# Exact 12-bit halves of the source tiles, one single-pass product for each, in the graph convolutions of a four-layer GNN + expert-FFN kernel; the gated pass's first loads issued one stage earlier

## The reference, cut to what matters

```
def _gcn_conv(h, row, col, norm, W, b, n_nodes):
    h = h @ W.T
    msg = h[row] * norm[:, None]               # norm = dinv[row] * dinv[col]
    out = jax.ops.segment_sum(msg, col, num_segments=n_nodes)
    return out + b
h = relu(_gcn_conv(x, row, col, norm, W1, b1, n_nodes))
h = relu(_gcn_conv(h, row, col, norm, W2, b2, n_nodes))
out = _gcn_conv(h, row, col, norm, W3, b3, n_nodes)
```

```
ei   = concatenate([x[src], edge_attr], axis=-1)        # 256 + 64 wide
core = maximum(ei @ W1 + b1, 0) @ W2 + b2
gate = sigmoid(ei @ Wg + bg)
agg  = segment_sum(gate * core, dst)
```

## Time and profile before

| | |
|---|---|
| median of three runs | 4353.53 us |
| the profiled execution | 4353.69 us, of which 4351.9 us span |
| busy: PE, PEld | 3722.1 us (86%), 2780.0 us (64%) |
| busy: DVE, ACT, POOL | 2239.8 us (51%), 1240.2 us (28%), 1958.0 us (45%) |
| granted TensorE clock, mean | 0.874 |
| convolutions, first product to last weigh | 1931.53 to 2824.52 us |
| gated pass, start of its block | 3094.8 us |

### The profile page before, as it was taken

One profiled execution on the slowest core, in us unless ns is written; L12 is line 12 of the kernel. 1 busy time (PEld: TensorE's weight loads), 2 busy tenths in 40 slices (PEclk: granted clock), 3 DMA queues, 4 the chain that ended last, 5 costly groups with the idle time before them and its releaser, 6 DMA issues. The chain is left out here.

```text
span 4351.9 us, 63004 instructions
## 1 busy us (share of the span) xinstructions
PE 3722.1 (86%) x19067; PEld 2780.0 (64%) x19067; DVE 2239.8 (51%) x6358; ACT 1240.2 (28%) x3588; POOL 1958.0 (45%) x2029
## 2 busy tenths in 40 slices
PE   3999992964887877849999999978899999998796
PEld 2666661543666666836566566554588888887696
DVE  6887787136555543242012122153577777778423
ACT  3777762210000012210000000021455555555331
POOL 2777766777777766740000000024354544442153
PEclk8999995985557577979999999987999999998698
DMA  7887850002333325745545554355455554442466
GB/s 231 240 227 213 229 142 14 9 3 86 106 106 106 105 61 160 233 148 150 152 136 153 149 146 138 110 144 140 146 146 143 143 143 144 144 143 87 150 211 206
DMA packets 424224, 613.68 MB, mean 141 GB/s; under 512 B 149417, under 2 KB 287794, under 8 KB 423634
## 3 DMA queue, kind: packets, MB, share of 16 engines
q1 hardware_dynamic: 310722, 327.46, 26.3%
q0 software_dynamic: 104112, 273.76, 21.7%
q10 hardware_dynamic: 9056, 8.43, 0.6%
HBM read 517.83 MB, written 91.59 MB: 140 GB/s over the span
## 5 line engine op out<-in xcount | busy, mean ns | idle before, releaser
L873 POOL DMA_INDIRECT eg_rows<-t_edge,src_i x416 | 394.1, 947 | 488.4 <-DVE eg_pre L1711 357.5
L1395 PE MATMUL ps<-cv_cells,xn 128*128 128x384 f32 (+2 forms) x1600 | 535.5, 493 | 60.0 <-DMA cv_cells<-t_cells 60.0
L1116 PE MATMUL ps<-sum_hot,sum_rows 128*128 128x128 f32 x1664 | 439.6, 421 | 170.2 <-DVE sum_hot L1095 92.5
L1116 PEld LDWEIGHTS ps<-sum_hot,sum_rows 128*128 128x128 f32 x1664 | 345.1, 294 | 264.8 <-DMA sum_rows<-t_row,src_i 171.3
L279 POOL DMA_INDIRECT t_cells<-times_seen,cell x416 | 414.4, 996 | 170.4 <-issue 126.2
L1395 PEld LDWEIGHTS ps<-cv_cells,xn 128*128 128x128 f32 x1600 | 304.5, 191 | 272.8 <-issue 61.0
L873 POOL DMA_INDIRECT ag_rows<-t_att,src_i x416 | 403.7, 970 | 138.1 <-issue 118.0
L873 POOL DMA_INDIRECT sum_rows<-t_row,src_i x416 | 393.9, 947 | 129.5 <-issue 120.0
L1663 PE MATMUL ps<-eg_w,eg_rT 128*128 128x256 f32 x1664 | 438.7, 386 | 1.9 <-ACT eg_rT L1681 1.9
L1711 DVE TENSOR_TENSOR eg_pre<-ps,eg_rows 128x512 f32<-128x512 f32 x416 | 283.4, 682 | 141.9 <-PE ps L1650 140.8
L1663 PEld LDWEIGHTS ps<-eg_w,eg_rT 128*128 128x128 f32 x1664 | 283.7, 190 | 57.9 <-issue 34.1
(11 more groups left out here) (412 smaller groups left out, 6409.7 us busy)
## 6 DMA issues: line engine op xcount, KB each, us to landing
cv_cells<-t_cells SPq DMA_DIRECT2D x225, 384.0 KB, 3.2
cv_cells<-t_cells SPq DMA_DIRECT2D x75, 448.0 KB, 3.3
xn<-in_L_ffn_W SPq DMA_DIRECT2D x57, 512.0 KB
t_cells<-zeros SPq DMA_DIRECT2D x17, 1664.0 KB
xn<-in_L_ffn_expert_w SPq DMA_DIRECT2D x110, 256.0 KB, 3.7
ag_trow<-t_dst SPq DMA_DIRECT2D x104, 256.0 KB
t_cells<-zeros POOLq DMA_DIRECT2D x8, 1664.0 KB, 23.3
eg_eaT<-in_edge_attr SPq DMA_DIRECT2D x208, 64.0 KB, 3.3
```

The costliest lines, as they stand in the source:

```text
L873: nc.gpsimd.indirect_dma_start(out=rows[:, j, :], out_offset=None, in_=table, in_offset=bass.IndirectOffsetOnAxis(ap=src_i[:, n:n + 1], ax ...
L1116: mm = nc.tensor.matmul(ps[:, j % BANKS, k * EC:(k + 1) * EC], lhs, hot[:, j, :], start=True, stop=True)
L1395: mm = nc.tensor.matmul(ps[:, bank(q, k, half), 0:at.stop - at.start], source(l)[:, s, k * 128:(k + 1) * 128], cells[:, n % CR, at], start ...
```

## The change

In the convolutions:

- ACT copies each source tile into a tile of type float32r (`high`, ring of four), which keeps the upper 12 bits of the mantissa. POOL subtracts that copy from the source tile and writes the rest, also as float32r (`low`). The two parts add up exactly to the value.
- PE multiplies `high` and `low` in turn with the counts, read as float32r; each source tile and quarter has eight products of the program where it had four.
- ACT now does this copy 300 times and its three copies of `cv_shared` between them. The waits for the source tile (`chain`) and for the copy of the shared part move: from PE to ACT, and to the start of quarter 1.
- POOL clears `featT` for layers 1 and 2 in eight pieces, between the subtractions of source tiles 17 to 24.
- `begin` of quarter 1 is 16 and was 14. The halves of the last quarter are 412 and 410 columns wide.

In the gated pass: the six loads of weights and biases and the first four of attributes are issued by SP in `collect_and_project`, behind the sixth store of `t_edge`; the tiles for them are kept through the stage before. The other attribute loads stand written out, where they were a loop.

```
+            high = sb("cv_high", [P, HR, D], F32R, c)      # HR = 4
+            low = sb("cv_low", [P, HR, D], F32R, c)
...
                 def _(pool):
-                    for l in range(LAYERS):
-                        if l > 0:
-                            pool.wait_ge(g.y_ready.sem, g.y_ready.at(NT * l))
-                        nc.gpsimd.memset(featT[:, :, 0:N], 0.0).then_inc(g.table_clear.sem, 1)
+                    nc.gpsimd.memset(featT[:, :, 0:N], 0.0).then_inc(g.table_clear.sem, CLEARS)
+                    for l, q, s, n in all_halves():
+                        pool.wait_ge(g.high_kept.sem, g.high_kept.at(n + 1))
+                        nc.gpsimd.tensor_tensor(low[:, n % HR, :], source(l)[:, s, :], high[:, n % HR, :].bitcast(F32), ALU.subtract).then_inc(g.low_kept.sem, 1)
+                        if l > 0 and q == 0 and CLEAR_AT <= s < CLEAR_AT + CLEARS:
+                            if s == CLEAR_AT:
+                                pool.wait_ge(g.y_ready.sem, g.y_ready.at(NT * l))
+                            c0 = (s - CLEAR_AT) * (N // CLEARS)
+                            nc.gpsimd.memset(featT[:, :, c0:c0 + N // CLEARS], 0.0).then_inc(g.table_clear.sem, 1)
...
                         for k in range(KD):
-                            for half in range(2):
-                                at = part(q, half)
-                                mm = nc.tensor.matmul(ps[:, bank(q, k, half), 0:at.stop - at.start], source(l)[:, s, k * 128:(k + 1) * 128],
-                                                      cells[:, n % CR, at], start=(s == 0), stop=(s == NT - 1))
+                            for which, split in enumerate((high, low)):
+                                if k == 0 and which == 0:
+                                    pe.wait_ge(g.high_kept.sem, g.high_kept.at(v + 1))
+                                elif k == 0:
+                                    pe.wait_ge(g.low_kept.sem, g.low_kept.at(v + 1))
+                                for half in range(2):
+                                    at = part(q, half)
+                                    mm = nc.tensor.matmul(ps[:, bank(q, k, half), 0:at.stop - at.start], split[:, v % HR, k * 128:(k + 1) * 128],
+                                                          cells[:, n % CR, at].bitcast(F32R), start=(s == 0 and which == 0), stop=(s == NT - 1 and which == 1))
...
-                            begin = 14 if q == 1 else 8
+                            begin = 16 if q == 1 else 8
...
                 def _(act):
+                    for l, q, s, n in all_halves():
+                        if n >= HR:
+                            ul, uq, us, _ = list(all_halves())[n - HR]
+                            act.wait_ge(g.used.sem, g.used.at(load_number(ul, uq, us) + 1))
+                        if l > 0 and q == 0:
+                            act.wait_ge(g.chain.sem, g.chain.at(2 * (NT * (l - 1) + s + 1)))
+                        nc.scalar.copy(high[:, n % HR, :], source(l)[:, s, :]).then_inc(g.high_kept.sem, 1)
...
                         sp.dma_start(t_edge[P * t:P * (t + 1), :], h[:, t % RING, :]).then_inc(store[t % RING].sem, 16)
+                        if t == RING:
+                            gated_loads(sp, *gated)
```

More of the change, by code:

```diff
@@ L198, in build_in @@
     store = [sig(f"row_store{j}") for j in range(RING)]
+    gated_w_in = sig("gated_weights_in")
+    attr_in = [sig(f"attributes_in{j}") for j in range(ER)]
     slot_stored = [sig(f"slot_stored{j}") for j in range(8)]
@@ L1442, in _ @@
                 def _(act):
[L1443 to L1447 removed]
+                    for l, q, s, n in all_halves():
[5 more added lines that the diff above has]
+                        nc.scalar.copy(high[:, n % HR, :], source(l)[:, s, :]).then_inc(g.high_kept.sem, 1)
+                        if q == 0 and s == NT - 1:
+                            act.wait_ge(g.used.sem, g.used.at(shared_load_number(l, NT // SP_LOT - 1) + 1))
+                            if l > 0:
+                                act.wait_ge(g.head_added.sem, g.head_added.at(128 * l))
+                            nc.scalar.copy(shared[:], ps[:, 4:6, 0:128]).then_inc(g.shared_kept.sem, 1)
                 @block.vector
@@ L1580, in collect_and_project, with edge_gated @@
             gath[i].passed(16 * RING)
-    def edge_gated(gb, gcol, bcol, wr, br):
-        DE = 64
+    def edge_gated(gated, gb, gcol, bcol, wr, br):
+        DE = ATTR
+        w1g, w2, b2, eaT = gated
         GE = 2 * ER
@@ L1624, in _ @@
                         sp.dma_start(bcol[:], io["L3_ffn_beta"].rearrange("(k p) -> p k", p=128)).then_inc(g.experts_in.sem, 16)
-                    def attributes(m, j, first):
-                        if not first:
-                            sp.wait_ge(g.pre_ready.sem, g.pre_ready.at(2 * (m - ER) + 2))
-                        sp.dma_start(eaT[:, j, :], io["edge_attr_64"][bass.ds(m, 1)].rearrange("m p e -> p (m e)")).then_inc(store[j].sem, 16)
-                    def body(i, first):
-                        for j in range(ER):
-                            attributes(ER * i + j, j, first)
-                    rounds(sp, PAIRS // ER, body)
+                    for m in range(ER, PAIRS):
+                        sp.wait_ge(g.pre_ready.sem, g.pre_ready.at(2 * (m - ER) + 2))
+                        attributes_in(sp, eaT, m)
                 @block.tensor
                 def _(pe):
-                    pe.wait_ge(g.loaded.sem, g.loaded.at(16 * NL))
+                    pe.wait_ge(gated_w_in.sem, gated_w_in.at(16 * GATED_WEIGHTS))
                     def attr_products(n, i, j, first):
@@ L1645, in attr_products @@
                         for pair in range(j // 2, j // 2 + ER // 2):
-                            pe.wait_ge(store[pair].sem, store[pair].at(16 * i + 16))
+                            pe.wait_ge(attr_in[pair].sem, attr_in[pair].at(16 * i + 16))
                             for c in range(2):
@@ L2579, in ffn1, with ffn2 @@
             collect_and_norm(pw)
-    def ffn2():
+    def ffn2(gated):
         E, H = 32, 64
@@ L2608, in ffn2, with ffn3 @@
             weights.close()
-            collect_and_project(place)
-    def ffn3():
+            collect_and_project(place, gated)
+    def ffn3(gated):
         E, H = 8, 512
@@ L2620, in ffn3 @@
             gb = sb("f3_gb", [P, 2, D], F32, c)
-            edge_gated(gb, gcol, bcol, wr, br)
+            edge_gated(gated, gb, gcol, bcol, wr, br)
             pw = sb("f3_pw", [P, 2, NT], F32, c)
@@ L2654, in attention, with last_layers @@
             att_finish(sums, own, shift, top)
+    def last_layers():
+        with ExitStack() as c:
+            gated = gated_tiles(c)
+            ffn2(gated)
+            ffn3(gated)
     stages = [
```

62 lines of the change are left out of this document (36 added, 26 removed).

## The result

The changed kernel takes 4074.29 us (median of four runs, 4071.72 to 4077.95), the kernel before 4350.67 us beside it: ratio 0.937 (95% interval 0.935 to 0.938), 276 us less. The forecast was 4057, range 4012 to 4100. The profiled execution took 4077.95 us with a span of 4076.2.

The account below looks back on a forecast made before the run. PE was taken to bound the convolutions and the gated pass. 4353.7 - 390.5 (products) + 104.7 (pauses) + 1.5 (start) - 13.5 (gated pass) + 1 (DVE held) = 4056.9, forecast 4057 us, range 4012 to 4100.

Parts of the forecast that it names:

- A: Convolutions: new products take one clock per column and PE waits for DVE once per layer; 4057 us, chance 0.80.
- B: Convolutions: new products take two clocks per column, source tiles 2.58 us as before; 4360 us, no change, chance 0.09.
- C: Convolutions: each new product takes four clocks per column, 645 ns in two instructions; 5130 us, chance 0.03.
- D: Convolutions: transfers set the pace, 1.40 us per 384 KB; up to +25 us, 4082, chance 0.08.
- Term 1: PE's products in the convolutions: 162.5 ns per 384 columns, 132.2 us per layer from 262.4; -390.5 us over three layers.
- The 170 ns: Slower case for a product in the convolutions, costing the kernel another 12 us or so.
- Term 2: PE's wait for DVE's additions before each layer's first weighing, lengthened by POOL's subtractions: 32.5 us per layer, +104.7 with slow clock.
- The slow clock: After each pause before the first weighing PE runs at 1.2 GHz for a while, costing 2.4 us per pause.
- Term 3: Start of the convolutions: PE waits for POOL's first subtraction, behind its first memset; +1.5 us.
- Hidden things: Convolutions: ACT's copy and POOL's subtraction, POOL's memset pieces and the loads of counts stay covered, costed at nothing.
- Term 4: Start of the gated pass: early loads end PE's wait for attributes, gathered rows then decide; -13.5 us, +1 for DVE held.

Follow-up runs that it names:

- e5: Changed kernel with only 4 of DVE's 128 additions of shared columns per layer: 0.926 of the kernel before, convolutions 538.3 us.
- e6: Changed kernel with the 768 columns of the first three quarters cut into 512 and 256: 0.944 of the kernel before, convolutions 627.3 us.
- e3: Changed kernel with a second ACT copy in place of POOL's subtraction, lower parts not computed: 0.942 of the kernel before, convolutions 590.9 us.
- e1: Changed kernel with one tiny POOL subtraction placed in idle time before the convolutions: 0.941 of the kernel before, convolutions 620.7 us.

## Why the prediction was right, and where its terms were off

The mechanism is A: one MATMUL per product, and one pause of PE per layer that DVE's additions set. B (322 ns) and C (645 ns) are ruled out by the pace, D by e5 and by the 5 us without transfers. The forecast for the stage was -284.3 us and -261.5 was measured. Term by term:

- **Term 1, the products: the step that was most off.** 162.5 ns per 384 columns took for granted that the 2.5 ns beside the columns stay 2.5 ns. It is 173.4, and 180.4 and 186.9 in the last quarter. Per layer 600 x 0.1734 + 100 x 0.1804 + 100 x 0.1869 = 140.8 us in place of 132.2: +25.6 over three layers. So against two instructions of 322.5 ns the gain is 3.7 to 1 and not 4 to 1. The 170 ns that I had put at the far end of it were still too fast. Where the 8% above one clock per column come from stays open: weight loads that take 173 ns, POOL and the transfers are ruled out, by e6, by e3 and by the 5 us without transfers; a fixed cost of some 13 ns per product isn't.
- **Term 2, the pause: right to 13 us.** From the end of the shared products (1984.8) to the first weighing (2042.36) it took 57.5 us, forecast 59.8. A subtraction costs DVE 9.3 / 21 = 0.44 us, not 0.55. With that and slower products in front, the pauses are 84.6 us in all where 97.5 were forecast. Of these 12.9 us, 5.5 are what the slower products of quarter 0's end take (21 x 8 x 10.9 ns per layer), and the pause gives them back; the rest is the smaller cost of the subtractions. The slow clock behind it was as taken (2.1 us up to the next weighing, 2.4 forecast). e3 shows the exclusive lock of the Trainium skill (SBUF — State Buffer, SBUF: two separate sides), a port pair that POOL or DVE holds for a whole instruction, by itself: additions of 164 ns without POOL's subtractions, up to 748 with them.
- **Term 3, the start: missed.** 10.56 us in place of 1.5. I counted POOL's first TENSOR_TENSOR at its 0.73 us. The trace of before held the hint, 8.1 us of "issue" ahead of L1608, but there it was covered and I read only the duration. e1 shows it.
- **Hidden things.** Behind the start PE waits for neither `cv_low` nor `cv_cells`; the chain of ACT and POOL, the memset pieces and the counts cost nothing, as said.
- **Term 4, the gated pass.** -12.1 in the block for -13.5, and +0.6 in the stage before for +1: the waiting moved to the gathered rows as said, but these let DVE start 4.8 us after their issue, not 3.2. DVE's first sum is 5.3 us behind PE's first product of the block, where the start to the sum was put at about 4.

Sum: +25.6 - 12.9 + 9.1 = 21.8 of the 22.8 us by which the stage missed. The errors had different signs: the pause had to give back 5.5 of the products' 25.6 us, by its mechanism, but that the subtractions cost less than taken was luck, and it kept the whole within 17 us. That the two parts hold the upper 12 bits of a value and the rest is the kernel's design; no run here measures how many bits a part keeps, and no time above rests on it.

## What to carry to other kernels

When the engine that bounds a stage becomes nearly twice as fast, ask what it had been covering: here 48 us of DVE work per layer had lain just under 49 us of PE's, and starting that work earlier, with the first TENSOR_TENSOR placed in idle time, gave 42 us more. Work moved to POOL is paid for by a DVE chain that works in SBUF beside it, so count POOL's instructions there. Before an engine gets a kind of instruction at a new place, look in the old trace for an "issue" gap ahead of its first one in the program.

## What the runs showed of the hardware

- A float32r product streams at 1.06 to 1.11 clocks per column at 2.4 GHz (116.5 ns for 256 columns, 173.4 for 384, 233.2 for 512), a float32 product at two instructions of 2.0 each (322.5 ns for 384). In the last quarter the pace was the same with the DMA engines busy 0.6 to 0.7 and with none busy.
- POOL's first TENSOR_TENSOR of the program starts 6.8 to 9.9 us late, once, in every trace here, behind a MODIFY_POOL_CONFIG; in e1 a one-column one takes the gap on itself.
- A DVE addition of 128 x 2 values takes 165 ns alone and up to 748 beside a POOL subtraction of 740 ns; a chain of them lost 0.32 to 0.45 us per subtraction.
